# Pair projections of an attention block from seven half-size products per couple of pairs, with weights in a ring

## The reference

```python
def ref(x, emb, W_emb, b_emb, g_norm, W_qkv, g_q, g_k, W_out):
    scale, shift = jnp.split(emb @ W_emb + b_emb, 2, axis=-1)
    xn = _rms_norm(x, g_norm) * (1.0 + scale) + shift
    qkv = (xn @ W_qkv).reshape(b, n, 3, h, d)
    q, k, v = ...                                  # each (b, h, n, d)
    q, k = _rms_norm(q, g_q), _rms_norm(k, g_k)
    attn = softmax(einsum('bhqd,bhkd->bhqk', q, k) * d ** -0.5)
    o = einsum('bhqk,bhkd->bhqd', attn, v).reshape(b, n, dim)
    return o + o @ W_out
out = x + ref(x, cond[:, None, :], ...)
```

## Time and profile before

| | before |
|---|---|
| time, median of 3 runs | 2278.11 us |
| the profiled execution's own time | 2278.89 us |
| its span | 2276.0 us |
| TensorE busy | 2256.2 us, 99% |
| VectorE busy | 1597.9 us, 70% |
| ScalarE busy | 1345.7 us, 59% |
| GpSimd busy | 651.7 us, 29% |
| DMA moved | 346.35 MB, mean 152 GB/s |

### The profile page before, as it was taken

The page is one execution under the profiler, slowest core; times in us unless marked ns, Lnnn a source line. Parts: engine busy times, 40 slices in busy tenths (PEclk is TensorE's granted clock), DMA queues, the critical chain, the costliest instruction groups (busy, mean ns, idle before and its releaser), DMA issues.

```text
span 2276.0 us, 36733 instructions
## 1 busy us (share of the span) xinstructions
PE 2256.2 (99%) x13392; PEld 2110.3 (93%) x13392; DVE 1597.9 (70%) x3284; ACT 1345.7 (59%) x3101; POOL 651.7 (29%) x880
## 2 busy tenths in 40 slices
PE   8999999999999999999999999999999999999999
PEld 4999989999999999999999999999999999999999
DVE  4898784787827778287872878738786487854875
ACT  4687772667616676176762667526674366743663
POOL 3444431324213241122312234122331223302220
PEclk9999999999999999999999999999999999999999
DMA  9544346422364332733236332362323723246331
GB/s 359 224 167 177 112 154 228 178 99 110 118 220 184 107 115 88 256 148 112 111 114 256 112 112 112 122 253 107 112 112 130 291 92 118 82 151 246 111 121 65
DMA packets 71269, 346.35 MB, mean 152 GB/s; under 512 B 7601, under 2 KB 43441, under 8 KB 47537
## 3 DMA queue, kind: packets, MB, share of 16 engines
q1 hardware_dynamic: 71088, 344.01, 41.2%
HBM read 293.65 MB, written 50.33 MB: 151 GB/s over the span
## 4 chain that ended last, share of the span: by engine, by line
PE 86%; DVE 8%; ACT 2%; issue 1%; POOL 0%; DMA 0%; ACTq 0%; DVEq 0%
PE proj_bank L502 18%; PE proj_bank L500 18%; PE proj_bank L501 18%; PE flip_bank L598 9%; PE pv_bank L609 5%; PE pv_bank L610 5%; PE score_bank L590 4%; PE score_bank L591 4%; PE flip_bank L553 2%; DVE probs L865 2%; DVE neg_max L859 2%; DVE pt_lo L869 2%; PE flip_bank L563 1%; ACT k_hi L700 1%; PE proj_bank L525 1%
## 5 line engine op out<-in xcount | busy, mean ns | idle before, releaser
L500 PE MATMUL proj_bank<-w_split,xn_hi 128*128 128x384 f32 x2048 | 700.0, 342 | 1.4 <-DVE res L907 0.8
L502 PE MATMUL proj_bank<-w_split,xn_lo 128*128 128x384 f32 x2048 | 688.5, 336 | 0.0
L501 PE MATMUL proj_bank<-w_split,xn_hi 128*128 128x384 f32 x2048 | 687.4, 336 | 0.0
L718 ACT ACTIVATE probs<-score_bank,neg_max 128x512 f32<-128x512 f32 x512 | 352.6, 691 | 213.5 <-DVE neg_max L859 211.2
L500 PEld LDWEIGHTS proj_bank<-w_split,xn_hi 128*128 128x128 f32 x2048 | 385.2, 188 | 18.1 <-DVE xn_lo L854 1.0
L501 PEld LDWEIGHTS proj_bank<-w_split,xn_hi 128*128 128x128 f32 x2048 | 385.5, 188 | 15.2
L724 ACT CAST pt_hi<-flip_bank 128x512 fp32r<-128x512 f32 x512 | 288.8, 591 | 182.0 <-PE flip_bank L598 91.1
L869 DVE TENSOR_TENSOR pt_lo<-flip_bank,pt_hi 128x512 fp32r<-128x512 f32 x512 | 339.9, 685 | 78.1 <-ACT pt_hi L724 75.9
L502 PEld LDWEIGHTS proj_bank<-w_split,xn_lo 128*128 128x128 f32 x2048 | 384.8, 188 | 0.0
L859 DVE TENSOR_REDUCE neg_max<-score_bank 128x1 f32<-128x512 f32 x512 | 341.3, 684 | 17.0 <-PE score_bank L591 13.0
L865 DVE TENSOR_SCALAR probs<-probs,row_inv 128x512 f32<-128x512 f32 x512 | 275.7, 539 | 18.1
(11 more groups left out here) (86 smaller groups left out, 3205.1 us busy)
## 6 DMA issues: line engine op xcount, KB each, us to landing
w_split<-w_store SPq DMA_DIRECT2D x140, 1536.0 KB, 7.0
w_store<-w_split SPq DMA_DIRECT2D x20, 1536.0 KB, 10.1
x_tile<-in_x SPq DMA_DIRECT2D x32, 512.0 KB, 11.0
w_raw<-in_w_qkv SPq DMA_DIRECT2D x16, 768.0 KB, 8.4
w_split<-w_store SPq DMA_DIRECT2D x12, 1024.0 KB, 5.1
w_raw<-in_x SPq DMA_DIRECT2D x56, 192.0 KB, 6.7
out<-w_raw SPq DMA_DIRECT2D x56, 192.0 KB, 1.9
emb_stage<-in_w_emb SPq DMA_DIRECT2D x5, 1024.0 KB, 10.6
```

The costliest lines, as they stand in the source:

```text
L500: nc.tensor.matmul(dst, a_hi, w_hi, start=(kt == 0), stop=False)
L501: nc.tensor.matmul(dst, a_hi, w_lo, start=False, stop=False)
L502: mm = nc.tensor.matmul(dst, a_lo, w_hi, start=False, stop=(kt == KT - 1))
L718: nc.scalar.activation(probs[h][:, i, :], score_bank[n % 2][:, :], ACT.Exp, bias=neg_max[:, n:n + 1], accum_out=row_sum[:, n:n + 1]).then_ ...
```

## The change

Two pairs are now a couple: their 768 columns and the 512 tokens of a batch make a product of two by two blocks, and it is made from seven block products in place of eight (Strassen's scheme in its form with 15 sums). With the activations' blocks y11 to y22 (halves of the channels, and tiles of tokens) the kernel forms y21+y22, y11 less that, and so on (VectorE, step G, four for each of two tile pairs, in place in `x_tile`); with the weights' blocks the sums w22-w12 and so on (step J, batch 0 only, half on VectorE and half on GpSimd, in place in the raw blocks). Each of the seven operands of both sides is split into high and low: 14 operands of 128x512 a batch in `xa_hi` and `xa_lo` (steps Y and, on GpSimd, X), and 14 units of weights a couple instead of 8 slices for each of two pairs (steps L).

A product j is computed for two token tiles i from 4 slices x 3 parts into `proj_bank[i]`; a step C is 2 slices, 6 matmuls of 384 columns, and 28 steps make a couple instead of 32. Products 1, 4 and 6 go on adding in the bank where the one ahead left its sum. The results leave PSUM by step E: for j 0 and 1 ScalarE copies them, for j 2 to 6 VectorE adds them to what has been formed before, into `u_part` and `stage`. So v is copied no more, the squares are taken from `stage`, and q and k are scaled there by GpSimd (step M), where VectorE had done it out of PSUM. T turns q and k into the score banks, no more into `flip_bank`, and waits for the last exponentials of the pair ahead. x is modulated in place, four of eight quarters by VectorE and four by ScalarE.

The output projection has four blocks of 256 columns in place of three. The two buffers of weights become a ring of 15 chunks of 2 KB per partition: a unit of two slices takes three chunks (768 KB) for a couple and two (512 KB) for the output, five couple units fit, and each is loaded as soon as those that lay in its chunks are used. The eight jobs of a batch run in the order of JOB_TURN. All order tables are written anew; HEAD now reaches to the scores of pair 11.

The core of the diff (the tables are left out; add_weights for GpSimd is that of VectorE with the other slice):

```diff
+OUT_W = 2 * P
+NOUT = D // OUT_W
+JOB_TURN = "0 P0 P1 1 P2 P3 2 3".split()
+OLDEST = 6
+COUPLE = 14
+OUT_UNITS = KT // 2
+CHUNKS = 15
...
+PRODUCTS = 7
+TILE_TURN = [(0, 2, 1, 3), (1, 3, 0, 2)]
...
+def all_jobs():
+
+    jobs = [("C", 0, 2 * g) for g in range(PAIRS // 2)]
+    for b in range(1, B):
+        jobs += [("P", b - 1, int(t[1])) if t[0] == "P" else ("C", b, 2 * int(t)) for t in JOB_TURN]
+    return jobs + [("P", B - 1, oc) for oc in range(NOUT)]
...
-        w_split = [sb(f"w_split{i}", [P, KT * 2 * QKV], F32R) for i in range(2)]
-        xn_hi = sb("xn_hi", [P, KT, T], F32R)
-        xn_lo = sb("xn_lo", [P, KT, T], F32R)
+        w_ring = sb("w_ring", [P, CHUNKS, 512], F32R)
+        xa_hi = sb("xa_hi", [P, PRODUCTS, KT // 2, T // 2], F32R)
+        xa_lo = sb("xa_lo", [P, PRODUCTS, KT // 2, T // 2], F32R)
...
-        qk_stage = sb("qk_stage", [P, TT, 2 * P])
-        v_stage = sb("v_stage", [P, 2, TT, P])
...
+        stage = sb("stage", [P, 2, TT, QKV])
...
+        def unit_space(engine, unit):
+
+            for last in KEPT[unit]:
+                job, k = last
+                if not ends_tile(last):
+                    engine.wait_ge(w_used, USED_NO[last] + 1)
+                else:
+                    engine.wait_ge(proj_done, TILES[job] + (k + 1 if job[0] == "C" else TT))
+                if is_fresh(job):
+                    n = SPLIT_NO[last]
+                    engine.wait_ge(w_stored[n % 8], 16 * (n // 8 + 1))
...
-            def product(job, slot, tt, piece, act_hi, act_lo):
-
-                w, n, fresh = buf(job), job_width(slot), is_fresh(job)
-                dst = proj_bank[tt % 2][:, 0:n]
-                if piece == 0:
-                    wait_past(pe, proj_drained, count(job) * TT + (tt - 1))
...
-                    mm = nc.tensor.matmul(dst, a_lo, w_hi, start=False, stop=(kt == KT - 1))
-                    if tt == TT - 1 and kt < KT - 1:
-                        mm.then_inc(w_used, 1)
...
+            def three_parts(dst, a_hi, a_lo, w, start, stop, shared=False):
+
+
+                nc.tensor.matmul(dst, a_hi, w[:, 0, :], start=start, stop=False, skip_group_check=shared)
+                nc.tensor.matmul(dst, a_hi, w[:, 1, :], start=False, stop=False, skip_group_check=shared)
+                return nc.tensor.matmul(dst, a_lo, w[:, 0, :], start=False, stop=stop, skip_group_check=shared)
+
+            def couple_product(job, n):
+
+                j, i, half = n // 4, n // 2 % 2, n % 2
+                unit = job, 2 * j + half
+                dst = proj_bank[i][:, 0:QKV]
+                if half == 0:
+                    if j == 0:
+                        wait_past(pe, proj_drained, DRAINED[job] + i - 1)
+                    elif j < 3:
+                        pe.wait_ge(proj_copied, COPIED[job] + 2 * (j - 1) + i + 1)
+                    else:
+                        pe.wait_ge(proj_drained, DRAINED[job] + 2 * (j - 3) + i + 1)
+                    if job[2] == 0:
+                        pe.wait_ge(operand_lo[i * PRODUCTS + j], job[1] + 1)
+                if i == 0:
+                    weights_there(unit)
+                for e in range(2):
+                    kt = 2 * half + e
+                    mm = three_parts(dst, operand(xa_hi, i, j)[:, kt, :], operand(xa_lo, i, j)[:, kt, :],
+                                     unit_view(unit)[:, e, :, :], kt == 0 and j not in (1, 4, 6), kt == 3, j != 2)
+                if half == 1:
+                    mm.then_inc(proj_done, 1)
+                elif i == 1:
+                    mm.then_inc(w_used, 1)
...
                     if kind == "T":
-                        wait_past(pe, flip_free, releases(order, u))
                         if n == 0:
-                            pe.wait_ge(proj_drained, count(pair_job(m, c, p)) * TT + TT)
+                            pe.wait_ge(qk_scaled, it * TT + TT)
+                        if it:
+                            pe.wait_ge(exp_done, (it - 1) * 8 + (6 + n + 1 + CREDIT))
                         for tt in range(TT):
-                            mm = nc.tensor.transpose(flip_bank[flip][:, tt * P:(tt + 1) * P],
-                                                     qk_stage[:, tt, n * P:(n + 1) * P], ident[:, :])
+                            mm = nc.tensor.transpose(score_bank[n][:, tt * P:(tt + 1) * P],
+                                                     stage[:, p % 2, tt, n * P:(n + 1) * P], ident[:, :])
+                        mm.then_inc(qk_turned, 1)
+                    elif kind == "X":
...
+            def add_weights(g, n):
+
+                kt = 2 * (n % 2)
+                w11, w21, w12, w22 = [block[:, kt, :] for block in raw_blocks]
+                done = g * 8
+                if n < 2:
+                    for q in range(4):
+                        dve.wait_ge(raw_loaded[q], 16 * (g + 1))
+                    dve.wait_ge(w_lo_even, SPLIT_NO[(("C", 0, 2 * g), n)] + 1)
+                    nc.vector.tensor_tensor(w12, w22, w12, ALU.subtract).then_inc(sums_even, 1)
+                    dve.wait_ge(sums_even, done + 2 * n + 1)
+                    nc.vector.tensor_tensor(w11, w12, w11, ALU.add).then_inc(sums_even, 1)
+                elif n < 4:
+                    dve.wait_ge(sums_even, done + 2 * (n - 2) + 2)
+                    dve.wait_ge(w_lo_even, SPLIT_NO[(("C", 0, 2 * g), n)] + 1)
+                    nc.vector.tensor_tensor(w21, w21, w11, ALU.subtract).then_inc(sums_even, 1)
+                else:
+                    dve.wait_ge(sums_even, done + 2 * (n - 4) + 2)
+                    dve.wait_ge(w_lo_even, SPLIT_NO[(("C", 0, 2 * g), n + 2)] + 1)
+                    nc.vector.tensor_tensor(w12, w22, w11, ALU.subtract).then_inc(sums_even, 1)
...
+            def evict(job, n):
+
+                j, i = divmod(n, 2)
+                it, done = job[1] * PAIRS + job[2], DRAINED[job]
+                dve.wait_ge(proj_done, TILES[job] + n + 1)
+                u2, u3 = stage[:, 1, 2 * i, :], stage[:, 1, 2 * i + 1, :]
+                if j == 2:
+                    dve.wait_ge(proj_copied, COPIED[job] + i + 1)
+                    if it:
+                        dve.wait_ge(qk_turned, (it - 1) * 2 + 2)
+                        dve.wait_ge(v_lo_done, (it - 1) * 2 + (2 + CREDIT))
+                    dst, other = u2, u_part[:, i, :]
+                elif j == 3:
+                    dve.wait_ge(proj_drained, done + i + 1)
+                    dst, other = u3, u2
+                elif j == 4:
+                    dst, other = stage[:, 0, 2 * i + 1, :], u2
+                elif j == 5:
+                    dve.wait_ge(proj_drained, done + 2 + i + 1)
+                    dst, other = u3, u3
+                else:
+                    dve.wait_ge(proj_drained, done + 4 + i + 1)
+                    dst, other = u2, u2
+                nc.vector.tensor_tensor(dst, proj_bank[i][:, 0:QKV], other, ALU.add).then_inc(proj_drained, 1)
...
+            def add_operand(b, n):
+
+                i, m = divmod(n, 4)
+                y11, y12, y21, y22 = [x_part(4 * i + e) for e in range(4)]
+                if m == 0:
+                    freed(dve, "X", 4 * i + 2, b)
+                    freed(dve, "X", 4 * i + 3, b)
+                    dve.wait_ge(operand_lo[i * PRODUCTS + 4], b + 1)
+                    dst, one, other, op = y22, y22, y21, ALU.add
+                elif m == 1:
+                    dve.wait_ge(operand_sum[4 * i], b + 1)
+                    freed(dve, "X", 4 * i, b)
+                    dst, one, other, op = y21, y11, y21, ALU.subtract
+                elif m == 2:
+                    dve.wait_ge(operand_sum[4 * i + 1], b + 1)
+                    dve.wait_ge(operand_lo[i * PRODUCTS], b + 1)
+                    dst, one, other, op = y11, y22, y11, ALU.subtract
+                else:
+                    dve.wait_ge(operand_sum[4 * i + 2], b + 1)
+                    dve.wait_ge(operand_lo[i * PRODUCTS + 1], b + 1)
+                    freed(dve, "X", 4 * i + 1, b)
+                    dst, one, other, op = y12, y12, y11, ALU.subtract
+                nc.vector.tensor_tensor(dst, one, other, op).then_inc(operand_sum[n], 1)
...
-                    elif kind == "M":
-                        if n == 0 and not (is_first(b) and p == 0):
-                            dve.wait_ge(flip_full, flip_at(order, b, "T", 1, p - 1)[0] + 1)
-                        dve.wait_ge(qk_rstd_done, it * TT + (n + 1))
-                        nc.vector.tensor_tensor(qk_stage[:, n, :].rearrange("p (h d) -> p h d", d=DH),
-                                                proj_bank[n % 2][:, 0:2 * P].rearrange("p (h d) -> p h d", d=DH),
-                                                qk_rstd[:, n, :].unsqueeze(2).to_broadcast([P, 4, DH]),
-                                                ALU.mult).then_inc(proj_drained, 1)
...
+                    elif kind == "M":
+                        pool.wait_ge(qk_rstd_done, it * TT + (n + 1))
```

(3 more changed lines are left out.)

1113 lines of the change are left out of this document (607 added, 506 removed).

## The result

The changed kernel takes 2258.99 us (median of 4 runs, 2257.81 to 2262.91), the kernel before 2277.75 us beside it: a ratio of 0.9917, 95% interval 0.9902 to 0.9933. It is 0.8% faster, where 2.1% were forecast (2230 us). The profiled execution took 2257.81 us, its span 2255.9.

The account below looks back on a forecast made before the run. TensorE was taken as the bound, with VectorE taking over in the first batch: 2278.9 - 123.2 = 2155.7, less 4, plus 64 there gives 2216, plus 9 and 5 gives 2230 us. Range 2172 to 2272, leaving out 2 in 10.

Parts of the forecast that it names:

- TensorE's saving, 123.2 us: TensorE, all batches: pair projections save 133.2 us, output projection gives 10.0 back, net 123.2 us.
- Middle batches and ring, 9 + 5 us: Added losses: 9 us (0 to 30) for slips with VectorE nearly full, 5 us (0 to 40) for the weight stream.
- VectorE's work up to 7S0, 274 us: First batch, 36 us to pair 7's first scores: VectorE has 274 us of work against TensorE's 218.
- The time around that work, 8 us: Start of first batch: chain of operand sum, ScalarE rounding and subtraction ahead of a product adds 8 us.
- Rival (a): First batch: TensorE stays the bound, loss 10 to 40 us; time 2155 to 2200, say 2175; chance 0.20.
- Rival (b): Every batch: TensorE waits for weight loads, 5 to 6 us a batch; time 2265 us; chance 0.13.
- Rival (c): Middle batches: GpSimd's blocking pushes VectorE over TensorE, some 10 us a batch; time 2308 us; chance 0.09.
- the rule on the shared way: SBUF access: VectorE's two-input or two-port instructions and GpSimd's exclude each other; sets upper ends, leaves the sum unchanged.
- Rival (d): First batch: idle pieces drop TensorE to 1.2 GHz in some stretches, 25 us more; time 2255 us; chance 0.08.
- VectorE over 90%: Sign of being right: VectorE busy in over 90% of the stretch up to pair 7's scores in batch 0.
- TensorE at 75 to 80%: Sign of being right: TensorE busy in about 75 to 80% of the stretch up to pair 7's scores, batch 0.
- a normalisation of 0.6 us: Sign of being right: VectorE's normalisation of the probabilities has a mean of 0.6 us.

Follow-up runs that it names:

- ring_light: Changed kernel loading only half of each unit of weights in batches 1 to 7 (wrong output): 2248.25 us against 2259.43 on the same chip.
- v_plus: Changed kernel with 52 extra, unused reductions on VectorE in batch 0, one ahead of each of its low parts of weights: 2271.19 us.
- n_light: Changed kernel with VectorE's normalisation of the probabilities in batch 0 cut to 16 columns (wrong output): 2244.95 us.
- v_light: Changed kernel with VectorE's half of the weights' low parts cut from 384 to 16 columns in batch 0 (wrong output): 2245.12 us.
- all_light: Changed kernel with VectorE's and GpSimd's low parts of weights and all weight sums cut to 16 columns in batch 0 (wrong output): 2227.30 us.
- m_vec: Changed kernel with batch 0's scaling of q and k moved from GpSimd back to VectorE, reading SBUF: 2288.16 us.
- pe_light: Changed kernel without the third of the three matmul parts in batch 0's pair projections, 38.9 us less TensorE work (less exact output): 2255.87 us.
- warm_start: Changed kernel with 116 extra identity turnings on TensorE at seven waits ahead of the scores of pair 0: 2253.77 us, and 2254.48 when repeated.
- warm: Changed kernel with 315 extra identity turnings on TensorE ahead of 24 waits in batch 0: 2265.04 us.

## Why the prediction was wrong, step by step

- **TensorE's saving, 123.2 us: right.** In the middle batches matmuls of 384 columns still start 0.17 us apart and those of 256 columns 0.12. From 7S0 on the sum had 123.2 - 18.7 - 9 - 5 = 90.5 us of gain; measured 89.2.
- **Middle batches and ring, 9 + 5 us: right in sum.** A middle batch takes 265.6 us against 263.1 of TensorE's work; of the 2.5 us half of the stream has some 1 (ring_light). VectorE is at 77%, forecast 80. GpSimd's share of a middle batch grew from 27 to 39% without harm there: the normalisation's mean went from 542 to 517 ns in a middle batch and from 539 to 543 over the whole run, where I had 600. The prediction's 359 GB/s is a mean over a slice of 57 us and no limit: the kernel before moves 370 over its first 36 us (last column below) and 426 between 6 and 18 us. The figure of about 358 that the prediction takes from the Trainium skill does not agree with this trace, in which one core is at work, and the measurement decides.

```profile
0.00:36.00 36.00, 29.41 (x66) 6.01 (x67) 7.38 (x10) 10.77 (x21) 9.55 (x20) 1.00 0.95 370
```

- **VectorE's work up to 7S0, 274 us: right in sum (271.7), by errors that cancel.** Weight sums 0.65 to 0.90 us by their line (0.80 taken), the weights' low parts 0.71 (0.80), sums of operands 0.83 (0.65), operands' low parts 1.33, normalisations 0.72 (0.54 and a blocking of 6 us in all). Against their bare medians of 0.49 to 0.69 the groups hold some 37 us of waiting inside instructions.
- **The time around that work, 8 us: the step that failed.** I took VectorE as full from 36 us to 7S0 and added 8 us for the chain at the start: 36 + 274 + 8 = 318. It stood still for 37.9 us (309.6 - 271.7), 30 more than I had, and its work was 2 us less than I had: 318 + 30 - 2 = 346, and 2230 + 28 = 2258 is the time of the profiled execution, 2257.81. VectorE waited in this stretch for results of TensorE and ScalarE and didn't reach 100%; the sum of its work was a floor, and I used it as the time. A warning stood in the earlier trace rows: in the same stretch of the kernel before VectorE stood still for 39.5 of 240.5 us. That 39.5 and 37.9 agree is in part chance, since there TensorE was full and VectorE had time to spare. The idle time is no constant either: it is 33.0 us in v_plus (324.4 - 291.4), 45.0 in n_light, 49.5 in v_light and 68.1 in all_light. It shrinks as VectorE's work grows, which is the price of about a half said in another way. Six runs show this price; why it is not the whole is not shown. It is not the amount of TensorE's work (39 us less: 0 to 3 us), nor that of ScalarE's casts (30 us less: nothing). The order of the steps may be it (each pair's scores stand behind the lump of 28 projection steps of its couple, where before they stood between them), or GpSimd's own queue. No run here wrote that order anew or cut GpSimd's work alone, and the cause stays open.
- **Rival (a), 2175:** fell; VectorE's work alone takes it to 308 us, not to 276. **Rival (b), ring:** 6 to 8 us for half of the stream where it had 35 for all; the middle batches of 265.6 us leave no room for its 5 to 6 us a batch. **Rival (c), slower:** the blocking is real (below) but does no harm in the middle batches. The part of the change that the rule on the shared way spoke against, the scalings on GpSimd, is worth 29 us in batch 0, as far as m_vec undoes it: it scales from SBUF, where the kernel before scaled out of PSUM.
- **Rival (d), the clock:** the row that it named came, 0.92 up to 7S0 (I had said 0.9), and half clock in 16% of 309.6 us makes TensorE's work some 25 us longer. That this is the loss of batch 0 is unlikely, as pe_light took 39 us of the same work away and gained 0 to 3. It was measured for the start alone, where warm_start brought the clock from 0.83 to 0.97 and 3 to 4 us came back. The Trainium skill, page "TensorE: Matmul & The Clock Gate", section "Terms", gives the loss by a clock held low as the time at the low clock times one less its share. By an estimate from that, the start lost 11 us in the changed kernel and 2 in warm_start, 9 apart. The runs show less than half of this, 2.6 us at the scores of pair 0 and 3.9 in the median. Behind pair 0 no run restored the clock.
- **What I had named as signs:** VectorE over 90%: 88%, and 91% behind the scores of pair 0; TensorE at 75 to 80%: 81%; a normalisation of 0.6 us: 0.543; 7S0 at 315 to 320: 345.6, the one that was far off.

## What to carry to other kernels

When work moves from the full engine to another one, the second engine's sum of work is the floor of a stretch and not its time. Look in the trace of before how long that engine stands still in the stretch and for whom: this tells that idle time will remain, though not how much of it. To learn which engine a stretch hangs on, cut one engine's work there by a known amount and see how far a mark moves (here by 0 to 0.1 us per us for TensorE, 0 for ScalarE's casts, about half for VectorE); its share of the chain of waits did not tell it. Take more than one trace of each version, as the mark itself moved by 3 us here. A low clock behind waits cost less than half of the matmul time that it added, where TensorE wasn't the engine that set the pace. And look at what an experiment adds beside what it is meant to add: warm's filling brought a wait of its own.

## What the runs showed of the hardware

**GpSimd holds up some of VectorE's instructions whatever their size.** A normalisation cut to 16 columns (n_light) still lasts up to 1.22 us; bare it lasts 0.235. And a reduction with one input of 128x384 from SBUF (v_plus) was never held up, while the subtraction with two inputs right behind it was (ns, least/median/most):

```profile
L1076 DVE TENSOR_SCALAR probs<-probs,row_inv x56: 233/235/1220, 103.2 to 333.3; 128x16 f32<-128x16 f32 x56
```
```profile
L911 DVE TENSOR_REDUCE extra<-w_raw x52: 532/543/553, 61.6 to 319.9; 128x1 f32<-128x384 f32 x52
```
```profile
L912 DVE TENSOR_TENSOR w_ring<-w_raw,w_ring x72: 407/548/1346, 22.0 to 486.4; 128x384 fp32r<-128x384 f32 x56, 128x256 fp32r<-128x256 f32 x16
```

In n_light GpSimd works beside two such short normalisations from 327.92 us on:

```profile
327.92 3.74 POOL L1179 TENSOR_TENSOR xa_lo<-x_tile,xa_hi 128x512 fp32r<-128x512 f32 x3 [4.18 <-ACT xa_hi L817]
...
329.24 1.22 DVE L1076 TENSOR_SCALAR probs<-probs,row_inv 128x16 f32<-128x16 f32 x1
...
330.56 1.12 DVE L1076 TENSOR_SCALAR probs<-probs,row_inv 128x16 f32<-128x16 f32 x1
```

This fits with v_light, where 31 us of VectorE's work were meant to go and 20.5 went: its low parts of 16 columns last 169 ns in the median, 350 in the mean and up to 1028. The Trainium skill, page "SBUF — State Buffer", section "Who interferes with whom", says that on this chip a reduction never contends with GpSimd, and that an instruction with two SBUF inputs (against one of GpSimd that reads SBUF) or in a two-port mode does; the three rows agree. The 52 reductions from SBUF ran beside GpSimd, which was busy in 206 of 324 us, at their bare length.
